# A two-layer decoder on one core: memsets, first key loads and context projections of the opening put elsewhere

## What is computed

```
x = x + L0_attn(ln(x))          # 16 heads of width 8, full softmax, with output projection
x = x + L0_xattn(ln(x), ctx)    # one head: K = ctx @ Wk + bk, V = ctx @ Wv + bv
x = x + L0_ffn(ln(x))           # gelu(x @ w1) @ w2, weighted
x = x + L1_attn(ln(x))          # one head, causal
x = x + L1_xattn(ln(x), ctx)    # 16 heads of width 8
x = x + L1_ffn(ln(x))           # light branch for all, heavy branch for 128 routed tokens
```

## Time and profile before

| what | us |
|---|---|
| median of 3 runs | 400.35 |
| lowest and highest run | 397.36, 402.74 |
| the profiled execution, its own time | 398.36 |
| its span, from the first to the last instruction | 396.6 |
| what lies around the span | 1.8 |
| mean granted TensorE clock | 0.991 |

### The profile page before, as it was taken

One profiled execution on the slowest core, in us unless ns is written; L12 is line 12 of the kernel. 1 busy time (PEld: TensorE's weight loads), 2 busy tenths in 40 slices (PEclk: granted clock), 3 DMA queues, 4 the chain that ended last, 5 costly groups with the idle time before them and its releaser, 6 DMA issues.

```text
span 396.6 us, 9589 instructions
## 1 busy us (share of the span) xinstructions
PE 353.2 (89%) x3246; PEld 210.9 (53%) x3246; DVE 315.2 (79%) x874; ACT 265.6 (67%) x594; POOL 160.4 (40%) x267
## 2 busy tenths in 40 slices
PE   6889999999999889994988968999889889989994
PEld 6766445454444368783456744444444434447564
DVE  7758899989998177888466658898988997479995
ACT  2425888888878847772715658887777887765751
POOL 8415544754400013247003575258667422370001
PEclk9989999999999999998999999999999999999999
DMA  7441242213350000001100121311311300000003
GB/s 222 121 111 38 76 126 67 61 48 107 86 162 2 2 0 3 0 2 41 39 2 1 49 66 49 83 48 36 81 36 48 82 2 3 2 1 2 1 2 106
DMA packets 35830, 20.00 MB, mean 50 GB/s; under 512 B 4150, under 2 KB 34790, under 8 KB 35782
## 3 DMA queue, kind: packets, MB, share of 16 engines
q1 hardware_dynamic: 34982, 17.81, 16.8%
q10 hardware_dynamic: 608, 1.18, 0.8%
q0 software_dynamic: 192, 0.39, 0.4%
HBM read 5.58 MB, written 1.05 MB: 17 GB/s over the span
## 4 chain that ended last, share of the span: by engine, by line
PE 67%; DVE 12%; ACT 7%; issue 6%; POOL 3%; DMA 2%; ACTq 0%; POOLq 0%; DVEq 0%
PE pv_ps L1370 14%; PE s_ps L1324 14%; PE s_ps L1427 4%; DVE negmax_sb L954 3%; PE prep_ps L1280 3%; PE s_ps L1450 3%; PE s_ps L1333 3%; ACT probT_sb L658 3%; PE s_ps L1663 3%; PE out_ps L1482 3%; PE prep_ps L1284 2%; PE s_ps L1510 2%; DVE xn_sb L938 2%; PE out_ps L1401 2%; PE s_ps L1467 2%
## 5 line engine op out<-in xcount | busy, mean ns | idle before, releaser
L954 DVE TENSOR_REDUCE negmax_sb<-s_ps 128x2 bf16<-128x512 f32 x256 | 163.9, 691 | 30.8 <-PE s_ps L1333 30.1
L658 ACT ACTIVATE probT_sb<-s_ps 128x512 f32<-128x512 f32 x256 | 143.3, 596 | 31.9 <-PE s_ps L1324 28.8
L1324 PE MATMUL s_ps<-stack_sb 63*128 63x256 bf16 x512 | 89.7, 273 | 11.7 <-ACT probT_sb L658 4.6
L1333 PE MATMUL s_ps<-stack_sb 62*128 62x256 bf16 x512 | 87.1, 275 | 3.3 <-DMA stack_sb<-parts_sb 1.9
L1370 PE MATMUL pv_ps<-probT_sb,v_aug_sb 128*32 128x256 f32 x1024 | 68.5, 385 | 0.5 <-ACT probT_sb L658 0.5
L1324 PEld LDWEIGHTS s_ps<-stack_sb 63*128 63x128 bf16 x512 | 30.8, 94 | 67.5 <-ACT probT_sb L658 38.1
L511 POOL TENSOR_SCALAR rstd_sb<-mv_sb 128x2 f32<-128x2 f32 x32 | 7.1, 223 | 100.6 <-DVE mv_sb L930 100.2
L1370 PEld LDWEIGHTS pv_ps<-probT_sb,v_aug_sb 128*32 128x32 f32 x1024 | 26.7, 109 | 25.4 <-issue 12.8
L1333 PEld LDWEIGHTS s_ps<-stack_sb 62*128 62x128 bf16 x512 | 29.7, 94 | 8.8 <-DVE negmax_sb L954 3.2
L681 ACT ACTIVATE qkf_sb<-prep_ps,b_qkv_sb 128x256 f32<-128x256 f32 x56 | 23.9, 470 | 12.5 <-PE prep_ps L1284 12.5
L938 DVE TENSOR_SCALAR xn_sb<-x_all_sb,mv_sb,rstd_sb 128x128 f32<-128x128 f32 x64 | 22.5, 443 | 3.4 <-POOL rstd_sb L513 3.2
(11 more groups left out here) (206 smaller groups left out, 653.6 us busy)
## 6 DMA issues: line engine op xcount, KB each, us to landing
stack_sb<-parts_sb SPq DMA_DIRECT2D x186, 64.0 KB, 2.1
x_all_sb<-x SPq DMA_DIRECT2D x4, 256.0 KB, 2.9
ctxT_sb<-ctxT ACTq DMA_DIRECT2D x2, 512.0 KB, 6.7
f_w_sb<-f_w SPq DMA_DIRECT2D x2, 512.0 KB, 4.2
out<-x_all_sb SPq DMA_DIRECT2D x4, 256.0 KB, 2.4
d_w_sb<-d_w SPq DMA_DIRECT2D x2, 320.0 KB, 3.6
w_att_sb<-w_att SPq DMA_DIRECT2D x2, 256.0 KB, 4.1
stack_sb<-maxrow_sb ACTq DMA_DIRECT2D x32, 4.0 KB
```

The costliest lines, as they stand in the source:

```text
L658: act.activation(probT[:, c % 8], s2_ps[c % 2][:, :, :], ACT.Exp, scale=DH ** -0.5).then_inc(exp_ready, 1)
L954: dve.tensor_reduce(negmax[:, n % 2, :, max_column(max_head(h))], first_bank(c)[:, :, :], axis=AX.X, op=ALU.max, negate=True).then_inc(max ...
L1324: i = pe.matmul(s2_ps[c % 2][:, k, :], stack[rows, s3, 1, h // 2, k * P:(k + 1) * P], stack[rows, s3, 0, h // 2, :], start=True, stop=True)
L1333: i = pe.matmul(first_bank(c)[:, k, :], stack[rows, s3, 0, hp, k * P:(k + 1) * P], stack[rows, s3, 1, hp, :], start=True, stop=True)
```

## The change

- **POOL**: the clearing of stack 1 waits until DVE has done both first layer norms (`xn_ready` 2). The clearing of stack 2 comes after the first key loads.
- **First keys**: POOL loads three of the six terms, ACT's queue the other three, after `v_copy(0)` at (-3, 15). ACT's three count on `stacked[0]`, so the thresholds change from a half to a quarter.
- **SP**: the row of ones of stack 2 is filled just ahead of the stack load of batch 2 instead of at the start.
- **DVE**: `prepare_v_aug` of slots 2 and 3 stands ahead of the first `row_max` of step -1 instead of at (-3, 3).
- **PE and ACT**: `KV_AT` puts one projection in step -3, four in step -2 and three in step -1 (before: three in step -2, all at its end, and five in step -1). The seven fillers of step -2 go.

```diff
-KV_AT = {-2: (15, 15, 15), -1: (1, 4, 7, 10, 13)}
+KV_AT = {-3: (9,), -2: (1, 6, 10, 15), -1: (4, 8, 12)}
...
-BUSY = {(-3, 0): 10, (-3, 5): 2, (-3, 9): 4, (-2, 0): 2, (-2, 5): 2, (-2, 9): 3, (-1, 4): 3, (-1, 10): 3,
+BUSY = {(-3, 0): 10, (-3, 5): 2, (-3, 9): 4, (-1, 4): 3, (-1, 10): 3,
         (0, 1): 1, (0, 2): 1, (0, 3): 1, (0, 4): 2}
...
             if n == 0:
-                eng.wait_ge(first_keys, STACKED // 2)
-            eng.wait_ge(stacked[n % 3], STACKED * (n // 3 + 1) - (STACKED // 2 if n % 3 == 0 else 0))
+                eng.wait_ge(first_keys, STACKED // 4)
+            eng.wait_ge(stacked[n % 3], STACKED * (n // 3 + 1) - (STACKED // 4 if n % 3 == 0 else 0))
...
-            for s3 in range(3):
+            for s3 in range(2):
                 fill_stack(s3)
...
+                    if i == -1:
+                        fill_stack(2)
                     if has(i + 3, lo):
                         load_stack(i + 3)
...
                 pool.wait_ge(parts_ready, 1)
-                for r, (jq, jk) in enumerate(TERMS):
-                    pool.dma_start(stack[r::DH, 0, 1], parts[:, 0, 1, jk, :]).then_inc(first_keys, 16)
+                for r in range(len(TERMS) // 2):
+                    pool.dma_start(stack[r::DH, 0, 1], parts[:, 0, 1, TERMS[r][1], :]).then_inc(first_keys, 16)
...
                         rstd_step_(1)
+                        pool.wait_ge(xn_ready, 2)
                         clear_stack(1)
+                        load_first_keys()
                         clear_stack(2)
-                        load_first_keys()
...
+            def load_first_keys():
+
+                act.wait_ge(parts_ready, 1)
+                for r in range(len(TERMS) // 2, len(TERMS)):
+                    act.dma_start(stack[r::DH, 0, 1], parts[:, 0, 1, TERMS[r][1], :]).then_inc(stacked[0], 16)
...
                             v_copy(i + 3)
+                        if (i, h) == (-3, 15):
+                            load_first_keys()
...
+                        if (i, h) == (-1, 0):
+                            prepare_v_aug(slice(2, 4), 2)
                         if has(i + 1, lo):
                             row_max(i + 1, h)
...
-                        if h == 3 and i == -3:
-                            prepare_v_aug(slice(2, 4), 2)
```

## The result

| | kernel before | changed kernel |
|---|---|---|
| median of 20 runs each, us | 398.86 | 401.28 |
| lowest and highest run | 396.37, 404.39 | 400.63, 405.60 |
| ratio of the runs, 95% interval | | 1.0072 (1.0051 to 1.0093) |
| profiled execution: own time, span | 398.36, 396.6 | 401.03, 399.2 |
| mean granted clock of it | 0.991 | 0.981 |

The change makes the kernel slower by 0.7%, 2 to 3.7 us by the interval. The forecast was 401.7 us, by +1.3; measured are 401.28 and +2.4 by the medians, or +2.9 by the ratio.

The account below looks back on a forecast made before the run. The PE, busy 89% of the span, bounds the kernel, so the opening costs what step 0's start moves: 36.5 instead of 35.20, +1.3 us. Added to the median of 400.35 that gives 401.7 us, range 397.8 to 404.6.

Parts of the forecast that it names:

- Items 1 and 2: DVE in the opening: second layer norm back at 0.60 us; batch 0's parts at 12.1 instead of 14.84, 2.75 earlier.
- Item 3: ACT in the opening: batch 1's q and k come at 18.6 us against 15.43, issues 1.8 and copies 1.5.
- the faster rival: Opening: ACT's queue issues the three key loads at no cost, step 0 at 33.9, -1.3 us (399.0 us); chance 0.25.
- Item 4: DVE before the row maxima: moved memset loses its idle time, first row maximum at 23.75 instead of 21.39, 2.35 later.
- Item 5: PE's clock in step -1: low for 3 us from 24.1, 1.6 us more work at half speed, 0.8 us lost.
- items 5 and 6: PE in step -1: with the clock loss and three projections instead of four, PE alone ready for step 0 at 35.7.
- item 7: Start of step 0: load of the maxima, landing taken as 1.5 us, arrives at 36.5, 0.8 past the PE.
- The one with the clock fallen already in step -2: Step -2: PE idling from 15.1 to 16.6 lowers its clock; step 0 at 38.4, +3.2, so 403.6 us; chance 0.15.

Follow-up runs that it names:

- run 2: Changed kernel with all six first key loads on POOL and none in ACT's queue: ratio 1.0109 to the kernel before.
- run 4: Changed kernel with the old places of the context projections and the old fillers: ratio 1.0031 to the kernel before.
- Run 1: Changed kernel with only the v_aug memset moved, to DVE's idle time ahead of the split of batch 1: ratio 1.0016 to the kernel before.
- run 3: Changed kernel with 16 filler matmuls in the PE's gap ahead of the fourth head of step -1: ratio 1.0034 to the kernel before.
- run 8: Changed kernel with memset in DVE's idle time, all first keys on POOL, POOL's later work held back, projections at new places: ratio 0.9876 to the kernel before.
- run 5: Kernel before with only POOL's wait and clearing order, SP's fill, and the memset put after the bias fold: ratio 1.0026 to the kernel before.
- run 7: Changed kernel with memset in DVE's idle time, all first keys on POOL, POOL's later work held back until batch 1's split: ratio 1.0036 to the kernel before.
- run 10: Kernel before with 20 filler matmuls in the PE's gap in the middle: ratio 0.9972 to the kernel before.
- 11: Kernel of run 8 with 20 filler matmuls in the PE's gap in the middle: ratio 0.9832 to the kernel before, median 393.53 us.

## Why the prediction was right

The sign came out, and so did the mechanism up to step 0; the size of one term did not, and the time came out in part by luck. The change itself was forecast at 1.3 us and measured at 2.4 by the medians, so I had about half of it. That 401.7 lies so near 401.28 is because the median of three from which I started, 400.35, was 1.5 above the 398.86 of 20 runs.

- **Items 1 and 2, right.** Layer norm 0.60. Parts of batch 0 at 11.5, which from the fold is what item 2 says (1.9 and 1.9).
- **Item 3, right.** ACT's loads stand at 0.65 to 0.68 each where 0.60 was taken; the first ran partly beside other work, as the faster rival had it for all three. The q and k of batch 1 were split from 7.93 after the fold; item 3 says 8.4. The loads cost batch 1 1.2 us (run 2) where 1.8 was taken, the projections 1.3 (run 4) where 1.5 was.
- **Item 4, right.** First maximum 13.40 after the fold, 13.55 forecast, with the memset directly ahead. Here two small errors cancel: batch 1 came 0.5 earlier than forecast, and from its split to the first maximum it took 5.5 us instead of 5.15, with 0.38 of idling ahead of the memset that I had left out. Run 1 shows that this place costs 2.3 us of the first maximum and 3.1 us of step 0.
- **Item 5, the term that was mis-sized.** I took a fall of the clock of 3 us, of which 2.4 lie behind the fillers' start: 1.2 us lost there, 0.8 more than before. It lasted from 22.1 to 28.9, with 4.7 us behind the fillers' start, and run 3 measures its price as 2.1 us. This is the main part of the difference between the 1.3 forecast for step 0 and the 2.15 found (from the fold): the PE alone was ready at 26.6 where items 5 and 6 give 25.5, and the gate of item 7 took back 0.3.
- **Item 7, right in kind.** Step 0 is released by the load of the maxima, which waits 0.52 after the PE is free (0.8 forecast), and lands 1.67 after its issue (1.5 taken). In run 8, where no projection's copies come between the maxima and their load, that wait is gone.
- **Not in the prediction.** The fall in the middle. I wrote that everything behind step 0 shifts with it. The work does, and the gap in the middle is equally long in both kernels; but how long the clock is low around it differs between executions, and so does what comes later. I started from an execution with the short fall, and took what lies behind step 0 as fixed.
- **The rivals.** The faster one needed the loads to be free; one of three nearly was. The one with the clock fallen already in step -2 didn't happen: the gap there was 1.21 us and the clock stayed at 1.00.

The absolute landmark flatters the forecast as well: step 0 at 36.74 for 36.5 is near only because this execution started 0.6 us earlier.

## What to carry to other kernels

A memset that is moved "off the path" has to go where its engine idles in the new schedule, not where it idled in the old: moving work forward shifts the idle time too, and here the hole was already filled by the split that had become late. Where two batches share an opening, getting the first one ready earlier gave nothing here until the second was earlier as well (run 5 against run 8). When one profiled execution is the base, see first where its mean clock stands among the runs. Before moving work on POOL, look at what DVE does at the new time, and count a PE gap not by its length but by the work that follows it at the lower clock.

## What the runs showed of the hardware

- **DVE and POOL hold each other up.** A 128x2048 memset on POOL takes 1.79 to 1.83 us whatever DVE does, and some DVE operations beside it are stretched until it ends. A cast went from 0.43 to 2.43 (run 5; it had even started 0.32 before the memset), a tensor_scalar pair from 0.60 to 1.88 (run 7). The row maxima, which read from PSUM, are not: three of them took 1.89 beside the memset of run 8 (20.40 to 22.20), as many as elsewhere. Beside POOL's bias adds both sides pay: two tensor_tensor of DVE went from 0.69 to 1.09 and from 0.68 to 1.21, the bias adds from 1.42 to 2.04 (run 2 against the changed kernel). The Trainium skill (GPSIMD Engine Reference, section 1, Specifications) names the access to SBUF that GpSimd shares with VectorE; run 7 agrees, since the split is back at 2.5 us with POOL moved away. That beside a memset DVE pays and POOL doesn't, and that it can cost 2 us in one cast, I hadn't expected.
- **A load from ACT's queue isn't free for ACT.** 64 KB loads occupied it for 0.65 to 0.68 us each in the changed kernel; only the first ran beside copies. The 4 KB load of the maxima took 1.08 us there, beside a pair of copies.
- **The same gap, different falls.** Around the same 5.26 us of idling in the middle the clock was low for 3.4 us in one execution and for 6.8 in the ten others without fillers there. The length of a gap alone doesn't tell whether a fall follows, either. The gaps of 1.93 us (kernel before), 1.48 (run 5) and 1.28 (run 4) in the opening had a fall behind them within 1.4 us, the 1.50 ahead of the fold matmul had none, and neither had the 2.15 in the middle of run 10. What tells them apart these runs don't show. Filling the gap removed the fall each time that a profile shows it (runs 3, 10 and 11).
